# Last layer of a four-layer kernel: the sum of fourth powers by TensorE from eight buffers instead of GpSimd's additions, and three rectified tiles

## The reference

```
def _rms_norm(x):
    eps = jnp.asarray(jnp.finfo(x.dtype).eps, x.dtype)
    ms = jnp.mean(jnp.square(x), axis=-1, keepdims=True)
    return x * jax.lax.rsqrt(ms + eps)
w1 = _ternary_weight(W_fc, GROUP)
h = jnp.einsum('bsd,hd->bsh', x, w1)
h = jnp.square(jax.nn.relu(h))
hn = _rms_norm(h)
w2 = _ternary_weight(W_proj, GROUP)
return jnp.einsum('bsh,dh->bsd', hn, w2)
```

## Time and profile before

| | us |
|---|---|
| median of 3 runs | 1992.72 (1991.88 to 1993.17) |
| the profiled execution | 1993.24 |
| its span, first to last instruction | 1991.4 |
| mean granted clock of TensorE, as a share of 2.4 GHz | 0.895 |
| busy: TensorE | 1521.4 (76%) |
| busy: VectorE | 1369.4 (69%) |
| busy: ScalarE | 1072.8 (54%) |
| busy: GpSimd | 962.0 (48%) |

### The profile page before, as it was taken

The page is one execution under the profiler, slowest core; times in us unless marked ns, Lnnn a source line. Parts: engine busy times, 40 slices in busy tenths (PEclk is TensorE's granted clock), DMA queues, the critical chain, the costliest instruction groups (busy, mean ns, idle before and its releaser), DMA issues. The chain is left out here.

```text
span 1991.4 us, 29193 instructions
## 1 busy us (share of the span) xinstructions
PE 1521.4 (76%) x8262; PEld 1000.8 (50%) x8324; DVE 1369.4 (69%) x3542; ACT 1072.8 (54%) x2293; POOL 962.0 (48%) x972
## 2 busy tenths in 40 slices
PE   4579898989898650597737878789999878863885
PEld 2313333333333240455625766678888667752563
DVE  4477777777777137343552799999999999846434
ACT  1106666666666600003002699999999999951311
POOL 5301332323332421032021599999999999830434
PEclk9859999999999975799868998889999889985998
DMA  2210010101010006000001000000000100000000
GB/s 92 99 41 24 18 33 17 32 17 31 18 27 7 1 0 230 1 1 1 1 32 35 1 1 1 1 1 1 1 1 1 43 1 1 1 1 0 11 11 21
DMA packets 32015, 42.68 MB, mean 21 GB/s; under 512 B 8328, under 2 KB 26656, under 8 KB 31648
## 3 DMA queue, kind: packets, MB, share of 16 engines
q1 hardware_dynamic: 31904, 41.36, 6.6%
HBM read 32.55 MB, written 8.39 MB: 21 GB/s over the span
## 5 line engine op out<-in xcount | busy, mean ns | idle before, releaser
L1724 POOL TENSOR_SCALAR c_R<-c_Z,c_negtau 128x256 f32<-128x256 f32 x519 | 589.2, 1170 | 86.7 <-DVE c_negtau L1793 58.0
L457 DVE TENSOR_REDUCE a_mpart<-a_nat 128x1 f32<-128x512 f32 (+3 forms) x640 | 378.0, 632 | 128.5 <-PE a_nat L578 83.1
L549 ACT ACTIVATE a_PT<-a_sc 128x512 f32<-128x512 f32 x576 | 316.9, 602 | 257.5 <-PE a_sc L611 173.6
L1681 ACT ACTIVATE c_R<-c_Z,c_negtau 128x256 f32<-128x256 f32 x1017 | 425.4, 516 | 3.4 <-DVE c_negtau L1793 1.7
L1760 DVE BATCH_NORM_STATS2 c_stat<-c_R 128x6 f32<-128x512 f32 x576 | 381.2, 678 | 1.1 <-ACT c_R L1681 0.6
L575 PE MATMUL a_nat<-KS,QS 96*128 96x512 bf16 (+3 forms) x768 | 253.5, 348 | 77.3 <-DVE a_mpart L457 43.0
L430 POOL TENSOR_SCALAR_AFFINE_SELECT a_PT<-a_PT 128x512 f32<-128x512 f32 x128 | 79.1, 636 | 406.1 <-ACT a_PT L549 406.1
L1611 PE MATMUL c_z<-mem_G,c_R 128*128 128x256 f32 x1024 | 246.5, 399 | 0.1
L1611 PEld LDWEIGHTS c_z<-mem_G,c_R 128*128 128x128 f32 x1024 | 206.1, 204 | 31.7 <-ACT c_Z L1669 1.7
L611 PE MATMUL a_sc<-QS,KS 128*128 128x512 bf16 (+3 forms) x706 | 194.1, 324 | 3.9 <-ACT a_PT L549 3.1
L1623 PE MATMUL c_T<-ident,c_R 128*128 128x128 f32 x768 | 117.2, 301 | 92.5 <-ACT c_R L1676 91.8
(11 more groups left out here) (329 smaller groups left out, 2066.3 us busy)
## 6 DMA issues: line engine op xcount, KB each, us to landing
qk_parts<-a_parts SPq DMA_DIRECT2D x4, 1536.0 KB, 5.9
QS<-qk_parts SPq DMA_DIRECT2D x192, 32.0 KB
KS<-qk_parts SPq DMA_DIRECT2D x192, 32.0 KB
X<-in_L_attn_x_dram SPq DMA_DIRECT2D x1, 2048.0 KB, 8.3
w_q<-in_L_ffn_wq_dram SPq DMA_DIRECT2D x1, 2048.0 KB, 11.5
w_o<-in_L_ffn_wo_dram SPq DMA_DIRECT2D x1, 2048.0 KB, 21.5
out_dram<-X SPq DMA_DIRECT2D x4, 512.0 KB, 3.0
QS<-a_msplit SPq DMA_DIRECT2D x96, 4.0 KB, 1.7
```

Source lines behind the costliest of these rows:

```text
L457: dve.tensor_reduce(mpart[:, b, j:j + cnt, i, k0 // 512], src, AX.X, ALU.max).then_inc(s_max, 1)
L549: act.activation(PT[:, n % 3, c, :], sc[:, u % 3, :], ACT.Exp, scale=SCALE0).then_inc(s_exp, 1)
L1681: act.activation(split(i, h) if r < NR else whole(i, h), Z[:, slot(i), h, :], ACT.Relu, bias=threshold(i, r, h)).then_inc(s_ra[r], 1)
L1724: pool.tensor_scalar(split(i, h) if r < NR else whole(i, h), Z[:, slot(i), h, :], threshold(i, r, h), 0.0, ALU.add, ALU.max).then_inc(s_rp ...
```

## The change

- GpSimd's 28 additions, the tile acc and its semaphore s_acc go.
- h2 gets eight buffers. ScalarE's Square writes tile n into h2[n], tile 0 too, and no longer waits for the additions.
- TensorE makes the sum in `second`: after y, for each of the four row tiles, eight matmuls of h2[u] by the column of ones add up in one PSUM column: 32 matmuls a group instead of 4. It waits for the eighth Square (s_h2) instead of the last addition.
- r gets three buffers, and Relu of tile u waits for the square of tile u-3 instead of u-2.

```
--- before.py
+++ after.py
@@ -2006,11 +2006,11 @@
         ps = lambda n, s: ctx.enter_context(nc.psum_tensor("d1_" + n, s, F32))
         mv, rstd = K.ffn_mv, K.ffn_rstd
         xn, xT = sb("xn", [P, GT, D]), sb("xT", [P, KC, GT * P])
-        r, hT, h2, acc = sb("r", [P, 2, 512]), sb("hT", [P, HC, 512]), sb("h2", [P, 2, 512]), sb("acc", [P, 512])
+        r, hT, h2 = sb("r", [P, 3, 512]), sb("hT", [P, HC, 512]), sb("h2", [P, HC, 512])
         ones, rs, y = sb("ones", [P, 1]), sb("rs", [P, GT]), sb("y", [P, GT, D])
         turned, h_ps, y_ps, ms_ps = ps("turned", [P, KC, 512]), ps("h", [P, 3, 512]), ps("y_", [P, GT, D]), ps("ms", [P, 512])
-        s_xn, s_T, s_xT, s_h, s_r, s_sq, s_h2, s_acc, s_y, s_ms, s_rs, s_ysc, s_out, s_cst = (
-            sem(n) for n in "xn T xT h r sq h2 acc y ms rs ysc out cst".split())
+        s_xn, s_T, s_xT, s_h, s_r, s_sq, s_h2, s_y, s_ms, s_rs, s_ysc, s_out, s_cst = (
+            sem(n) for n in "xn T xT h r sq h2 y ms rs ysc out cst".split())
         tail = add_normalised(nc, ctx, K, "d1t", sem)
         block = ctx.enter_context(nc.Block())
 
@@ -2031,12 +2031,6 @@
         def _(pool):
             pool.memset(ones[:], 1.0).then_inc(s_cst, 1)
             def in_order(g):
-                for u in range(1, HC):
-                    pool.wait_ge(s_h2, HC * g + u + 1)
-                    if u >= 2:
-                        pool.wait_ge(s_acc, (HC - 1) * g + u - 1)
-                    pool.tensor_tensor(acc[:], acc[:], h2[:, u % 2, :], ALU.add).then_inc(s_acc, 1)
-
                 pool.wait_ge(s_rs, 2 * g + 1)
                 pool.tensor_tensor(rs[:], rs[:], K.mhalf[:, 0:GT], ALU.pow).then_inc(s_rs, 1)
                 tail.gpsimd(pool, g)
@@ -2060,7 +2054,7 @@
                 dve.wait_ge(s_y, g)
                 for u in range(HC):
                     dve.wait_ge(s_r, HC * g + u + 1)
-                    dve.tensor_tensor(hT[:, u, :], r[:, u % 2, :], r[:, u % 2, :], ALU.mult).then_inc(s_sq, 1)
+                    dve.tensor_tensor(hT[:, u, :], r[:, u % 3, :], r[:, u % 3, :], ALU.mult).then_inc(s_sq, 1)
 
             def outputs(g):
                 dve.wait_ge(s_y, g + 1)
@@ -2100,16 +2094,13 @@
                     if u < HC:
                         act.wait_ge(s_h, HC * g + u + 1)
 
-                        if u >= 2:
-                            act.wait_ge(s_sq, HC * g + u - 1)
-                        act.activation(r[:, u % 2, :], h_ps[:, u % 3, :], ACT.Relu).then_inc(s_r, 1)
+                        if u >= 3:
+                            act.wait_ge(s_sq, HC * g + u - 2)
+                        act.activation(r[:, u % 3, :], h_ps[:, u % 3, :], ACT.Relu).then_inc(s_r, 1)
                     if u >= 1:
                         n = u - 1
                         act.wait_ge(s_sq, HC * g + n + 1)
-
-                        if n >= 3:
-                            act.wait_ge(s_acc, (HC - 1) * g + n - 2)
-                        act.activation(h2[:, n % 2, :] if n else acc[:], hT[:, n, :], ACT.Square).then_inc(s_h2, 1)
+                        act.activation(h2[:, n, :], hT[:, n, :], ACT.Square).then_inc(s_h2, 1)
 
             copy_x(0)
             def in_order(g):
@@ -2150,10 +2141,12 @@
                         ins = pe.matmul(y_ps[:, k, :], hT[:, u, k * P:(k + 1) * P], K.W2T[:, u, :], start=(u == 0),
                                         stop=(u == HC - 1))
                 ins.then_inc(s_y, 1)
-                pe.wait_ge(s_acc, (HC - 1) * (g + 1))
+                pe.wait_ge(s_h2, HC * (g + 1))
                 pe.wait_ge(s_rs, 2 * g)
                 for k in range(GT):
-                    ins = pe.matmul(ms_ps[:, k:k + 1], acc[:, k * P:(k + 1) * P], ones[:], start=True, stop=True)
+                    for u in range(HC):
+                        ins = pe.matmul(ms_ps[:, k:k + 1], h2[:, u, k * P:(k + 1) * P], ones[:], start=(u == 0),
+                                        stop=(u == HC - 1))
                 ins.then_inc(s_ms, 1)
 
             pe.wait_ge(s_cst, 1)
```

More of the change, by code:

```diff
@@ L2033, in in_order @@
             def in_order(g):
[L2034 to L2038, removed]
                 pool.wait_ge(s_rs, 2 * g + 1)
```

## The result

| | us |
|---|---|
| before, median on the same chip | 1992.95 (1991.88 to 1995.08) |
| changed, median | 2021.41 (2019.71 to 2022.96) |
| ratio, 95% interval | 1.0141 (1.0124 to 1.0159) |
| changed, the profiled execution | 2022.65 (span 2020.9, mean granted clock 0.888) |

The change makes the kernel 28 us slower; 2019.4 had been forecast. The first view is TensorE's timeline in the last layer, the counterpart of the earlier trace rows. Its columns are the start, the duration, then line, operation and count; the bracket is the idle time ahead.

The account below looks back on a forecast made before the run. It took TensorE's second layer and d_ms, with VectorE's d_rs and tail behind, to bound the kernel. From 1993.24, +36.0 sums, -6.1 relief, +0.7 late start, -3.9 restarts gave 2019.9, median 2019.4; range 2009.5 to 2025.0.

Parts of the forecast that it names:

- the sum: Last layer, all terms together: +36.0 - 6.1 + 0.7 - 3.9 = +26.7 us against the profiled execution.
- The sums by TensorE: d_ms behind d_y_: 64 instructions a group instead of 8, 9.8 us each group, 36.0 us more in four groups.
- the 3.8 taken: d_ms stretch: the granted clock was to fall to half 3.8 us after the stretch starts.
- the boldest step: d_ms stretch: judged like a pause, so the clock falls to half level partway; this forecast was put at 0.68.
- The full-level rival: d_ms stretch: the clock stays full, +17.9 us, 2010.6 us in all; chance 0.20.
- The relief of GpSimd's additions: Last layer: VectorE's squares freed and d_y_ spared its half-level start, 6.1 us less, mostly in the last group.
- The restarts: TensorE's tiles behind d_ms: half-level start hidden in groups two and three, 0.7 us late in the last; 3.9 saved.
- at 2.5 us I take it kept: TensorE's pause before tile six: shortened to about 2.5 us it keeps the clock, saving restarts of 1.7 and 2.2 us.
- The third tile: ScalarE's queue: the third r buffer brings nothing, since Square(0) stands before relu(2) and waits for VectorE's first square.
- The free-instruction rival: One-column instructions behind d_y_ nearly free, only the 6.1 us relief left: 1986.6 us; chance 0.04.

Follow-up runs that it names:

- e1: Changed kernel with the 256 d_ms instructions spread in pieces of 16, each behind d_y_ of its row tile; 2012.69 us, ratio 1.0095.
- e2: Changed kernel with the column of ones made 128 wide, same instructions in the same places; 2015.09 us, ratio 1.0105.
- e4: Changed kernel with TensorE summing only the first of the eight h2 tiles, 8 instructions a group; 1988.16 us, ratio 0.9972.
- e9: Changed kernel with h2 and the ones in bf16 and Square lagging two tiles behind Relu; 1983.23 us, ratio 0.9938.
- e5: Changed kernel with the third rectified tile undone: two buffers for r and the old wait; 2020.60 us, ratio 1.0131.
- e7: Changed kernel with ScalarE's Square lagging two tiles behind Relu instead of one; 2017.38 us, ratio 1.0119.
- e3: Changed kernel with each one-column matmul placed behind the d_y_ matmul of the same tiles; 2024.33 us, ratio 1.0161; run again 2014.49 us.
- e8: Changed kernel with h2 and the column of ones in bf16, 32 instructions a group; 1986.91 us, ratio 0.9962.

## Why the prediction was right

- **The sign and the size.** 2019.4 was forecast, 2021.41 measured. By the two profiles the layer grew by 26.9 us (163.9 to 190.8), and the sum had said 26.7. The other 2.6 us of the 29.5 between the two spans lie ahead of the layer, in work that the change doesn't touch. So close an agreement is partly luck: the sums took 1.6 us more than said, and the first group happened to take 1.6 less (last point). By the medians the change costs 28.5 us, 1.8 more than the sum.
- **The sums by TensorE** were to take 9.8 us a group. They took 10.92, 11.23, 9.12 and 9.70: 41.0 in all, 37.6 more than before where 36.0 was said. The level fell 2.8, 2.5, 4.8 and 4.3 us after their start, 3.6 on average against the 3.8 taken. The 3.8 was an average over pauses that ranged from 2.2 to 5.1, carried over to a stretch of another kind; that it fits is no more than the rows allow. That the level would fall in such a stretch was the boldest step, put at 0.68; e1 and e2 show that it does and what it depends on: with the same instructions spread out, or with 128 columns in place of one, it stays at 1.00.
- **The full-level rival**, 2010.6, is what e1 measures with the level kept: 2012.69. So of the layer's 26.9 us, 18.9 are left with the level kept, and 8.0 (9 to 10 by the comparison at e1) are what the level costs net. The four sums alone lose more by it, 41.0 against 27.2 us; the shorter pauses and the restarts at the full level give a part of it back.
- **The relief of GpSimd's additions** was worked out as 6.1 us and measured as 6.1 in the layer (e4), 5.6 by the ratio; the parts, 0.6, 3.4 and 2.0, were 0.6, 3.5 and 2.0. The 0.1 us of the third group can't be told from noise.
- **The restarts.** The half-level start of the next tiles was hidden by VectorE's tail in groups two and three, the pauses shrank to 1.45 and 2.23 us (2.5 said), and the level held in this profile: from the end of d_ms to d_y_ it is 19.88 and 20.34 us, against 22.18 and 22.63, so 2.3 us less in each, as said. In the last group it is 18.42 against 20.82: 2.4 less, where 3.4 - 0.7 = 2.7 was said. The step "at 2.5 us I take it kept" was lucky: the pauses came out shorter, because the half-level start cost more (the 20 instructions took 11.60 and 11.28 us; 8.83 + 2.2 is 11.0, not the 10.8 of the prediction), and where a pause did last 2.50 us (e9) or 3.00 (e5), the level was lost.
- **The third tile** brought nothing (e5), for the reason given: order within ScalarE's queue, not buffers. With the order changed (e7) TensorE does one tile more before it pauses.
- **The free-instruction rival** fell for fp32 (0.107 us) and e3 shows that mixing doesn't save it. In bf16 (e8) an instruction does cost only 0.025 us, just under the 0.027 from which this rival was to decide. But that bound was for 224 added instructions, which at 0.025 would cost 5.6 us and leave nearly nothing of the relief; e8 is clearly faster than before because it also has half as many, 32 a group.
- **What it had no term for** is the first group: 1.6 us less from the start of its first tiles to d_y_ (16.97 against 18.57), because the level rose sooner there.

## What to carry to other kernels

A matmul that moves one column isn't free: in fp32 each of its two instructions took 0.106 us, about what the same instruction took with 128 columns (0.112 in e2), with the weight loads back to back. Put such sums in bf16 where the accuracy allows, or sum elsewhere first. Don't let a long row of them stand alone on the path: here it lost the full clock after 2.5 to 4.8 us. If it must be there, break it up with dense work. And before a buffer is added, read the order of the queue that fills it: here an instruction in front of it waited for the very thing that the buffer was meant to get around.

## What the runs showed that I had not expected

- Moving 128 columns instead of one made the same 64 instructions faster, 7.14 us against 9.1 to 11.2, because the granted clock stayed 1.00.
- One-column bf16 instructions follow one another every 0.025 us, a quarter of the fp32 price, and there is one for each matmul where fp32 has two: 0.80 us for 32 matmuls against 6.8.
- The interleaved kernel has executions 17 us longer than its others (three of ten), with a lower mean clock; the kernel before showed none in the same batches. Its cause is open.
